# A three-stage vision tower on one core: a transposed group of values ahead of its features, and states and x on other byte offsets

## The reference

```
t = unfold3(x, stride 1)            # 27 features for each of 224*224 tokens
t = performer(t)                    # stage 1 of the kernel, out: 64 channels
t = unfold3(t, stride 2)            # 576 features, 112*112 tokens
t = performer(t)                    # stage 2, out: 64 channels
h = unfold3(t, stride 2) @ proj_w.T + proj_b          # 768 features, 56*56 tokens
                                    # stage 3: everything from here on
n = layernorm(h);  Bp, Cp = n@W_B, n@W_C;  d = softplus(n@W_D + p_Delta)
for each token t, channel c, state s (16 of them):
    a = exp(d*A);  b = (a - A)/(d*A) * d * Bp         # A is negative
    H[c,s] = a*H[c,s] + b*n[c];  y[c] = sum_s Cp[s]*H[c,s]
h = h + y
h = h + expert_mlp(layernorm(h))    # 8 experts, one per token, gelu

performer(x):  k, q, v = split(layernorm(x) @ W.T)
               kp = exp(k.w - |k|^2/2), qp likewise   # 32 features
               y = qp . (sum_t v kp) / (qp . sum kp);  y = v + proj(y);  y + mlp(layernorm(y))
```

## Time and profile before

| | us |
|---|---|
| median of three runs | 8710.51 |
| the profiled execution's own time | 8720.43 |
| its span, first to last instruction | 8718.7 |

### The profile page before, as it was taken

The page is one execution under the profiler, slowest core; times in us unless marked ns, Lnnn a source line. Parts: engine busy times, 40 slices in busy tenths (PEclk is TensorE's granted clock), DMA queues, the critical chain, the costliest instruction groups (busy, mean ns, idle before and its releaser), DMA issues.

```text
span 8718.7 us, 87074 instructions
## 1 busy us (share of the span) xinstructions
PE 7548.6 (87%) x31228; PEld 3143.8 (36%) x31228; DVE 6212.0 (71%) x6601; ACT 4308.2 (49%) x7753; POOL 5969.5 (68%) x2484
## 2 busy tenths in 40 slices
PE   8999999979999964888878888887888888888887
PEld 5444444334443321333333333333333333333333
DVE  2566666822333338888888888888888888888884
ACT  3666666833444424444544444455444445544442
POOL 0111111267666409998998999899999989999994
PEclk9999999989999976999988999988889999889988
DMA  1111111244444323323323332232333323233321
GB/s 38 38 43 45 44 44 36 51 99 100 98 101 101 66 63 106 104 95 110 114 97 121 116 105 100 100 124 95 119 107 114 104 95 124 100 107 119 114 102 52
DMA packets 356921, 786.65 MB, mean 90 GB/s; under 512 B 70437, under 2 KB 282870, under 8 KB 349000
## 3 DMA queue, kind: packets, MB, share of 16 engines
q1 hardware_dynamic: 320440, 690.78, 26.0%
q0 software_dynamic: 21712, 51.75, 2.3%
q10 hardware_dynamic: 14336, 38.54, 1.3%
HBM read 597.39 MB, written 183.35 MB: 90 GB/s over the span
## 4 chain that ended last, share of the span: by engine, by line
PE 35%; DVE 15%; ACT 6%; issue 5%; POOL 3%; DMA 0%; SPq 0%; DVEq 0%; ACTq 0%; POOLq 0%
PE ps L1644 8%; DVE v L1997 7%; PE ps L1752 6%; DVE v L1988 6%; PE ps L1651 6%; PE ps L1649 5%; PE ps L1690 3%; ACT ps L1879 3%; PE ps L1640 2%; PE ps L1755 2%; PE ps L1753 2%; POOL v L1599 1%; POOL v L1611 1%; PE ps L1694 1%; DVE dl L1978 1%
## 5 line engine op out<-in xcount | busy, mean ns | idle before, releaser
L1997 DVE TENSOR_TENSOR_SCAN v<-ps,v 128x898 f32<-128x898 f32 x1344 | 2725.3, 2028 | 92.3
L1611 POOL TENSOR_TENSOR v<-v,ct 128x1792 f32<-128x1792 f32 x672 | 2472.4, 3679 | 442.1 <-ACT st L1840 442.1
L1599 POOL TENSOR_TENSOR v<-xr,bt 128x1792 f32<-128x1792 f32 x672 | 2471.2, 3678 | 95.9 <-DMA xr<-h_by_channel 95.9
L1879 ACT ACTIVATE ps<-dr,aa 128x448 f32<-128x448 f32 x2688 | 1585.7, 627 | 1535.6 <-DVE v L1997 1518.3
L1988 DVE SCALAR_TENSOR_TENSOR v<-ps,aa,v 128x448 f32<-128x448 f32 x2688 | 1690.5, 671 | 548.1 <-ACT ps L1879 537.4
L236 POOL DMA_DIRECT2D tokens<-ob x448 | 235.3, 532 | 1534.2 <-DVE ob L563 1491.2
L1752 PE MATMUL ps<-w_or_w,gm 128*112 128x384 f32 x1792 | 716.6, 549 | 371.3 <-DVE gm L2074 278.8
L1690 PE MATMUL ps<-v,dg 128*32 128x448 f32 x5376 | 703.9, 598 | 203.6 <-POOL v L1611 109.1
L1752 PEld LDWEIGHTS ps<-w_or_w,gm 128*112 128x112 f32 x1792 | 332.8, 196 | 767.3 <-DVE gm L2074 320.5
L1644 PE MATMUL ps<-h,w_or_w 128*128 128x448 f32 x1344 | 537.2, 550 | 15.3 <-DVE gm L2041 15.3
L1805 ACT ACTIVATE h<-ps,pbias 128x448 f32<-128x448 f32 x168 | 106.2, 632 | 722.2 <-PE ps L1651 722.2
(11 more groups left out here) (322 smaller groups left out, 11960.5 us busy)
## 6 DMA issues: line engine op xcount, KB each, us to landing
xr<-h_by_channel SPq DMA_DIRECT2D x168, 896.0 KB, 7.3
dr<-delta_by_channel SPq DMA_DIRECT2D x168, 896.0 KB, 6.2
x<-tokens SPq DMA_DIRECT2D x252, 224.0 KB, 5.3
tokens<-ob POOLq DMA_DIRECT2D x448, 112.0 KB, 2.4
w_or_w<-in_w SPq DMA_DIRECT2D x29, 1536.0 KB, 6.4
w_or_w<-centred_w SPq DMA_DIRECT2D x27, 1536.0 KB, 6.5
h_by_channel<-h SPq DMA_DIRECT2D x112, 336.0 KB, 10.9
delta_by_channel<-dl SPq DMA_DIRECT2D x112, 336.0 KB, 5.1
```

What stands on the lines that cost most here:

```text
L1599: tt(v[:, n % RING, :, 1:T + 1], xr[:, dc % 2, 1:].rearrange("p (i t) -> p i t", i=4), bt[:, q:q + 1, :].to_broadcast([128, 4, T]), ALU.mu ...
L1611: tt(v[:, n % RING, :, 1:T + 1], v[:, n % RING, :, 1:T + 1], ct[:, q:q + 1, :].to_broadcast([128, 4, T]), ALU.mult).then_inc(s_cm, 1)
L1879: fn(decay(g), dr[:, dc % 2, g, :], ACT.Exp, scale=aa[:, 4 * k + g:4 * k + g + 1]).then_inc(s_a, 1)
L1997: nc.vector.tensor_tensor_scan(row, flat[:, 1024 * pair:1024 * pair + 2 * T + 2], row, 0.0, ALU.mult, ALU.add).then_inc(s_sc, 1)
```

## The change

There are two parts. In stage 2 the four matmuls that transpose the values of a pair stand first, then comes the wait for the features, and then the four that transpose the features; places in PSUM, operands and counts of instructions stay. In stage 3 the row of a group in `v` and the distance of two groups in PSUM grow from T+1 to GW = T+4 columns, the worked columns start two in instead of one, and the first state stands in column 1; `xr` becomes one tensor of 8*T+2 columns, in which x starts two columns in and the halves lie 4*T columns apart. So all four groups of v, both halves of x and all decays start 8 bytes past a multiple of 16. The scan's row starts at column 1 and has 901 columns, three unused ones between the groups. The unused columns of v are set to zero once, by two memsets more on POOL, and three engines wait for a count of 8 in place of 6 before the stage's loop. Seven one-column tensors become columns of one tensor, `small3`, which makes room.

```diff
 def transposes(n):
     own = half[1 - n % 2]
     pe.wait_ge(s_vn, n + 1)
     if n + 1 < NP:
         pe.wait_ge(s_va, n + 2)
+    for ch in range(NCH):
+        cols = slice(ch * CH, ch * CH + CH)
+        at = 256 * (ch % 2)
+        mm(ps[0:CH, 3 + ch // 2, at:at + 128], vp[:, n % RV, cols], ident[:, :], start=True, stop=True)
     pe.wait_ge(s_kp, 2 * (n + 1))
     for ch in range(NCH):
         cols = slice(ch * CH, ch * CH + CH)
-        o = ps[0:CH, 3 + ch // 2, 256 * (ch % 2):256 * (ch % 2) + 192]
-        mm(o[:, 0:128], vp[:, n % RV, cols], ident[:, :], start=True, stop=True)
-        last = mm(o[:, 128:192], kp[own, cols], ident[own, own], start=True, stop=True)
+        at = 256 * (ch % 2) + 128
+        last = mm(ps[0:CH, 3 + ch // 2, at:at + 64], kp[own, cols], ident[own, own], start=True, stop=True)
     last.then_inc(s_tr, 1)
...
+GW = T + 4
...
 def decay(g):
-    at = g // 2 * 1024 + g % 2 * (T + 1)
-    return flat[:, at + 1:at + T + 1]
+    at = g // 2 * 1024 + g % 2 * GW
+    return flat[:, at + 2:at + T + 2]
...
-xr = sb("xr", [128, 2, 4 * T + 1])
+xr = sb("xr", [128, 8 * T + 2])[:, 2:].rearrange("p (a t) -> p a t", a=2)
...
-v = sb("v3", [128, RING, 4, T + 1])
+v = sb("v3", [128, RING, 4, GW])
...
-tt(v[:, n % RING, :, 1:T + 1], xr[:, dc % 2, 1:]..., bt[...], ALU.mult)
+tt(v[:, n % RING, :, 2:T + 2], xr[:, dc % 2, :]..., bt[...], ALU.mult)
...
-row = v[:, n % RING, 2 * pair:2 * pair + 2, :].rearrange("p g t -> p (g t)")
+row = v[:, n % RING, 2 * pair:2 * pair + 2, :].rearrange("p g t -> p (g t)")[:, 1:GW + T + 2]
...
-nc.vector.tensor_tensor_scan(row, flat[:, 1024 * pair:1024 * pair + 2 * T + 2], row, 0.0, ALU.mult,
+nc.vector.tensor_tensor_scan(row, flat[:, 1024 * pair + 1:1024 * pair + GW + T + 2], row, 0.0, ALU.mult,
...
+pool.memset(v[:, :, :, T + 2:GW], 0.0).then_inc(s_set, 1)
+pool.memset(v[:, :, :, 0:1], 0.0).then_inc(s_set, 1)
...
-fn(st[:, 4 * k:4 * k + 4], v[:, n % RING, :, T], ACT.Copy).then_inc(s_st, 1)
+fn(st[:, 4 * k:4 * k + 4], v[:, n % RING, :, T + 1], ACT.Copy).then_inc(s_st, 1)
...
-fn(v[:, n % RING, :, 0], st[:, 4 * k:4 * k + 4], ACT.Copy,
+fn(v[:, n % RING, :, 1], st[:, 4 * k:4 * k + 4], ACT.Copy,
```

More of the change, by code:

```diff
@@ L1307, in decay @@
         def decay(g):
-            at = g // 2 * 1024 + g % 2 * (T + 1)
-            return flat[:, at + 1:at + T + 1]
+            at = g // 2 * 1024 + g % 2 * GW
+            return flat[:, at + 2:at + T + 2]
         def decays(pair):
-            row = flat[:, 1024 * pair:1024 * pair + 2 * T + 2]
-            return row.rearrange("p (g t) -> p g t", g=2)[:, :, 1:T + 1]
+            row = flat[:, 1024 * pair:1024 * pair + 2 * GW]
+            return row.rearrange("p (g t) -> p g t", g=2)[:, :, 2:T + 2]
         ident = sb("ident3", [128, 128])
@@ L1318, in tail @@
         desc = sb("desc", [CH, NCH, NX])
-        eps = sb("eps3", [128, 1])
-        e8 = sb("e8", [128, 1])
-        cap = sb("cap", [128, 1])
+        small = sb("small3", [128, 8])
+        eps = small[:, 0:1]
+        e8 = small[:, 1:2]
+        cap = small[:, 2:3]
         wpa = sb("wpa", [128, 3, D])
@@ L1326, in tail @@
         pbias = sb("pbias", [128, DC])
-        pm = sb("pm", [128, 1])
-        mub = sb("mub", [128, 1])
+        pm = small[:, 3:4]
+        mub = small[:, 4:5]
         wbc = sb("wbc", [128, DC, 48])
         wz = sb("wz", [128, DC, 128])
-        bbc = sb("bbc", [128, 1])
+        bbc = small[:, 5:6]
         pd = sb("pd", [128, DC])
         pc = sb("pc", [128, DC])
-        bd = sb("bd", [128, 1])
+        bd = small[:, 6:7]
         aa = sb("aa", [128, 4 * STEPS])
@@ L1511, in spread @@
                 after(sp, s_v, read)
-                sp.dma_start(xr[:, dc % 2, 1:],
+                sp.dma_start(xr[:, dc % 2, :],
                              bass.AP(xd.tensor, at, src)).then_inc(s_xr[dc % 2], 16)
@@ L1539, in _ @@
             sp.dma_start(w1, w["w1"]).then_inc(s_wv, 16)
-            sp.wait_ge(s_set, 6)
+            sp.wait_ge(s_set, 8)
             load_x(0)
@@ L1598, in weigh_in @@
                 after(pool, s_ns, n + 1 - RING)
-                tt(v[:, n % RING, :, 1:T + 1], xr[:, dc % 2, 1:].rearrange("p (i t) -> p i t", i=4), bt[:, q:q + 1, :].to_broadcast([128, 4, T]),
+                tt(v[:, n % RING, :, 2:T + 2], xr[:, dc % 2, :].rearrange("p (i t) -> p i t", i=4), bt[:, q:q + 1, :].to_broadcast([128, 4, T]),
                    ALU.mult).then_inc(s_v, 1)
@@ L1610, in weigh_out @@
                 pool.wait_ge(s_st, others(n))
-                tt(v[:, n % RING, :, 1:T + 1], v[:, n % RING, :, 1:T + 1], ct[:, q:q + 1, :].to_broadcast([128, 4, T]),
+                tt(v[:, n % RING, :, 2:T + 2], v[:, n % RING, :, 2:T + 2], ct[:, q:q + 1, :].to_broadcast([128, 4, T]),
                    ALU.mult).then_inc(s_cm, 1)
@@ L1689, in step @@
                 for g in range(4):
-                    last = mm(ps[32 * g:32 * g + 32, YB, 0:T], dg[:, 4 * k + g, :], v[:, n % RING, g, 1:T + 1],
+                    last = mm(ps[32 * g:32 * g + 32, YB, 0:T], dg[:, 4 * k + g, :], v[:, n % RING, g, 2:T + 2],
                               start=(q == 0), stop=False)
@@ L1922, in _ @@
             act.wait_ge(s_pd, 16)
-            act.wait_ge(s_set, 6)
+            act.wait_ge(s_set, 8)
             act.preload_act_table_set(BOTH)
@@ L1986, in weigh @@
                 dve.wait_ge(s_a, 4 * n + g // 2 * 2 + 2)
-                row = v[:, n % RING, g, 1:T + 1]
+                row = v[:, n % RING, g, 2:T + 2]
                 stt(row, decay(g), aa[:, 4 * k + g:4 * k + g + 1], row, ALU.subtract, ALU.mult).then_inc(s_wt, 1)
@@ L2007, in own_scan @@
                     dve.wait_ge(s_wt, 4 * n + g + 1)
-                    nc.vector.tensor_tensor_scan(decay(g), decay(g), v[:, n % RING, g, 1:T + 1],
+                    nc.vector.tensor_tensor_scan(decay(g), decay(g), v[:, n % RING, g, 2:T + 2],
                                                  0.0 if first else st[:, 4 * k + g:4 * k + g + 1], ALU.mult,
@@ L2013, in own_scan @@
                 dve.wait_ge(s_sp, 4 * owned(n) + 2 * pair - 2)
-                tt(v[:, n % RING, 2 * pair:2 * pair + 2, 1:T + 1], decays(pair),
+                tt(v[:, n % RING, 2 * pair:2 * pair + 2, 2:T + 2], decays(pair),
                    ct[:, k % Q:k % Q + 1, :].to_broadcast([128, 2, T]), ALU.mult).then_inc(s_cv, 1)
@@ L2084, in _ @@
             nc.vector.memset(ps[:, 0:AR, :], 0.0).then_inc(s_set, 1)
-            dve.wait_ge(s_set, 6)
+            dve.wait_ge(s_set, 8)
             dve.wait_ge(s_pd, 5)
```

## The result

The changed kernel takes **8673.57 us**, the median of 5 runs (8669.5 to 8674.95), beside 8710.51 for the kernel before: ratio 0.9955, interval 0.9940 to 0.9969. It is faster, by 37 us and not by 71: inside the range on record, 8608 to 8682, but outside the range of the forecast as worked out, 8622 to 8656. The profiled execution took 8669.5 us, its span is 8667.7, its mean granted clock 0.916 (before 0.918).

A forecast was written before the change was run, and what follows sets the result against it. PE was taken to bound stage 2; in stage 3 the chain, mostly PE, with POOL setting the pace for 271 us. Terms -54 - 20 + 3 = -71 us gave 8640 us for the median, range 8608 to 8682.

The forecast's parts named there:

- Transposes, -54: Stage 2's loop: grouping passes of one kind saves 0.96 us in each of 56 iterations, 54 us, all on PE's path.
- POOL, -20: Stage 3, first unit and start of the last: both multiplications at 3.38 us shorten POOL's path by 20 us.
- 271 us in which POOL sets the pace: Stage 3: 187 us in the first unit plus 84 at the last's start, where the chain runs through POOL's multiplies.
- DVE and ACT, +3: Stage 3's chain: scan +1.8 us, weighting L1988 +3.5, decays L1879 -2.3, together +3 us.
- middle units unchanged within 1 us: Sign to look for in the profile after: a unit in the middle of stage 3 keeps its length within 1 us.
- 10 us either way: Stage 3: the shifted start might move low clock stretches by 0.4 us in each of 26 units; only in the range.
- half of the transposes' gain lost: Case behind the range's upper end: stage 2 gains only half, giving 8667 us, with 10 us added for the clock.
- POOL gains nothing: Rival, stage 3: the new places undo what gave L1599 its two speeds; time 8660 us, chance 6%.
- The scan pays for its odd start: Rival, stage 3: DVE's scan from column 1 takes 0.37 us more, 100 us on the chain; 8740 us, chance 4%.
- My reading, multiples of 8: POOL's multiplications in stage 3: rows starting on a multiple of 8 bytes take 3.38 us, others 3.99.

The follow-up runs named there:

- 904 columns: The changed kernel with its scan over all 904 columns of two groups in place of 901: 8679.67 us, ratio 0.9947.
- pairs kernel: Kernel before plus regrouped transposes, x 8 bytes past 16, states in pairs of groups T+1 apart: 8668.22 us; with four extra matmuls before stage 3's projection, 8667.18.

## Why the prediction was half right

**Transposes, -54: right.** Measured -51.5 by the runs, and in the trace it takes 1118.9 us from the first pass of values to the last of features (1852.9 to 2971.8) where it took 1173.9 (1857.4 to 3031.3), 55.0 less. With the wait left where it was it takes 1119.8, so about 1 us at most is the order's, and the rest comes from passes of one kind standing together. The two kinds differ in the rows of their weights (128 and 64) and in their moving operand (128 and 64 columns); which of these counts no run separates. By the rule in the Trainium skill that the prediction weighed ("TensorE: Matmul & The Clock Gate", "Step-by-step: what each phase is for"; loads pulled ahead, so no gain) this part would have brought nothing. The trace does not agree for these passes. The features' run, estimated from a line with only 8 moving columns, was met too (0.93 us). One slip without effect: with 0.10 between the ends the term's best case is 57 us, not 58.

**POOL, -20: a term of the sum that was mis-sized.** The speeds were right (3.36 us, forecast 3.38, though from a wrong reading, below), the gain on the path was not. It gave 8.3 us in the first two units and nothing in the last. "271 us in which POOL sets the pace" took a share of the chain for a gain. The chain names what came last; how far behind it the next one was, the chain doesn't say. In the last unit that was next to nothing: in both kernels its first six steps already run at DVE's pace of 6.53 or 6.54 us. The chain before, near the end of the earlier trace rows's stretch, and the chain after at the same place:

```profile
8493.53 3.94 POOL v L1599
8497.49 1.29 DVE v L1988 x2
8498.82 0.04 issue
8498.87 2.03 DVE v L1997
```
```profile
8439.04 2.03 DVE v L2004
8441.08 1.18 DVE v L1995 x2
8442.45 1.90 issue
8445.00 1.29 DVE v L1995 x2
```

From the unit's first scan the weighting starts at 8497.49 - 8438.48 = 59.01 us before and at 8445.00 - 8386.19 = 58.81 after, both behind the eighteenth scan of the unit. A whole stretch of POOL on the chain hid 0.2 us. In the first unit the table gives the whole curve. A step of POOL is 7.69, 7.36, 7.04 or 6.72 us (the sum of its two multiplications); over 24 steps each stage of that is some 7.8 us, and unit 0 answers with 7.0, then 3.9, then nothing. After that the chain is DVE's (the kernel after, 3239 to 3427 us, unit 0 and the start of unit 1):

```profile
by line: DVE v L2004 28.9%; DVE v L1995 26.2%; issue 18.2%; ACT ps L1886 4.9%; PE ps L1656 3.9%; PE ps L1658 3.0%; PE ps L1651 2.5%; DVE dl L1985 2.0%; PE ps L1697 1.9%; PE ps L1647 1.7%; ACT dl L1839 1.4%; ACT dl L1837 1.4%; ACT dl L1832 0
```

The prediction set the floor at DVE's step of 6.53 and allowed 2 us for DVE's other work; unit 0 is 164.1 us, 7.4 over 24 steps of 6.53. What the last unit's end costs (280.2 to 281.8 in all kernels) follows no layout.

**DVE and ACT, +3, and "middle units unchanged within 1 us": the unit is right by that bound, but 0.53 us times 25 is 13.** The scan was priced by its share of the chain, +1.8 us. If all 48 of a unit count, that is 0.25 us a unit, 6 us in 25; L1879 did not get faster, and L1988 is within 1 ns of before. The other 7 us or more are on PE, as follows. Three stretches of one unit each before, and three after; the clock is the first figure behind the engines:

```profile
3841.36:4031.84 190.48, 160.19 (x571) 64.02 (x564) 167.62 (x174) 93.45 (x200) 174.73 (x49) 0.91 0.32 109
4031.84:4223.70 191.86, 161.11 (x554) 64.26 (x556) 167.66 (x174) 93.53 (x200) 174.72 (x49) 0.89 0.32 109
4223.70:4414.17 190.47, 160.14 (x571) 64.00 (x564) 167.63 (x174) 93.47 (x201) 174.72 (x49) 0.91 0.32 109
```
```profile
3775.77:3968.72 192.95, 162.41 (x554) 64.40 (x546) 167.92 (x174) 93.49 (x200) 160.04 (x48) 0.89 0.32 108
3968.72:4160.50 191.78, 161.48 (x578) 64.73 (x578) 167.84 (x175) 93.63 (x201) 159.98 (x48) 0.91 0.32 108
4160.50:4352.54 192.04, 161.19 (x554) 64.23 (x556) 167.92 (x174) 93.58 (x200) 159.96 (x48) 0.89 0.32 108
```

A unit takes about 190.5, 191.9 or 193 us. Before, 8 of 25 are of the short kind and 3 of the long; after, 2 and 7. The mean clock of a whole unit does not sort them: 191.78 us has 0.91 like 190.48, and 192.95 has 0.89 like 191.86. What sorts out the long ones is the MLP's line. Its eight passes have two prices, 4.53 and 2.77 us; the granted clock in these two stretches is 0.62 and 1.00 (the figure behind PE and weight loads), so the dear one lies in part at the lower of the clock's two levels (1.2 and 2.4 GHz), and 4.53 x 0.62 = 2.81 leaves next to nothing for another cause:

```profile
5941.11:5945.64 4.53, 4.53 (x8) 1.96 (x8) 0.62 0.81 239
5948.19:5950.96 2.77, 2.76 (x8) 1.26 (x8) 1.00 0.00 0
```

The line alone in three units running of the kernel before, the middle one long, and then over the middle units, L1752 before and L1759 after:

```profile
4414.17:4606.02 191.85, 24.92 (x62) 11.38 (x60) 0.89 0.32 108
4606.02:4798.97 192.95, 27.84 (x64) 12.59 (x64) 0.89 0.31 108
4798.97:4990.78 191.81, 25.98 (x67) 12.29 (x68) 0.91 0.32 108
```
```profile
3649.46:8438.48 4789.02, 642.00 (x1601) 297.76 (x1600) 0.90 0.32 108
```
```profile
3583.83:8386.19 4802.36, 652.19 (x1601) 301.37 (x1600) 0.90 0.32 108
```

The same passes take 10.2 us more in all. Through the 14 kernels of the table the line's time and the number of long units rise together, and the middle unit with them, from 638.8 us with 2 long units to 655.4 with 8. So the greater part of the lengthening, 10.2 of 13.3 us, is this line's passes at their dear price. It is not the amount of time at the lower level: with 904 columns the trace's clock records have 38.6 us a unit there, before 38.9 and after 40.1, and PE is busy for 4033 us, 3 more than before, yet the line has 654.1 and the unit is the longest. What counts is which work falls on the low stretches.

What makes it so is shown only in part. Every kernel with 898 or 899 columns has 191.44 to 191.81 a unit and 2 to 5 long ones, every one with 901 or more 191.98 to 192.25 and 6 to 8, with POOL slow or fast and the stage shifted or not. So it goes with the longer scan, or with the T+4 distance that always comes with it. But kernels of the same scan length differ by up to 0.37 us a unit too, more than the 0.28 that the scans' own time leaves of the 0.53, and each has one trace. Why 5 ns a scan should make long units is argued only: a unit that is 0.25 us longer can put its passes elsewhere against the low stretches. The 904 columns, 0.16 us more where the scans alone would be 0.38, show no fixed price for a column. The prediction had this effect as "10 us either way" and left it out of the sum.

In the traces POOL's 12 us too few and the middle's 10 too many make most of the 20 us between -71 and -51; the other 14 of the missing 34 are the distance of the two profiled executions from their medians (9.9 and 4.1). That the time still fell into the range is in part luck: its upper end was made from half of the transposes' gain lost and 10 us for the clock, and the first of these did not happen.

**Open.** The pairs kernel has 191.81 and 191.72 with 898 columns, the six other kernels with that length 191.44 to 191.71. In the trace this is the MLP's line again (647.1 us for before's 642.0), and before's own layout reaches 191.71 with the transposes regrouped. Whether the states' place or the faster second multiplication brings it was not separated from chance.

**Rivals.** "POOL gains nothing" was refuted as a mechanism (3.36 us), yet in the time it is the nearest: it had 8660, and the whole of stage 3's part is +8. The Trainium skill's 16-byte lines ("SBUF — State Buffer", "Specifications (TRN2)"), counted over a row, would have made both starts equal; the runs have 4.01 and 3.36. "The scan pays for its odd start" is refuted: from 901 columns on column 1, 2.033 us, from 901 on column 0, 2.035.

## What to carry to other kernels

Where PE is the bound, try matmuls of one kind in one run instead of two kinds by turns: here it was worth 0.96 us for every sixteen passes. A share of the chain is a bound, not a price: before an engine's gain is counted there, look at how late the second releaser is, and in a loop of 25 equal units price even 5 ns for each instruction of the engine that paces it. Where an edit has a part that pays and a part that costs, take the first alone: x with its one half moved by 4 bytes has most of what stage 3's part gained in the first two units and none of the longer middle, and with the transposes it made the kernel with the lowest ratio, 8655 us, 0.9928.

## What the runs showed of the hardware

- GpSimd's multiplication of 1792 columns with rows of 448 depends on where the *read* rows start against 16 bytes: all at 4 past 4.01 us, all at 8 past 3.36, by turns 8 and 12 past 3.36, by turns 8 and 0 past 3.68. So 0 and 4 past are slow (2 x 3.68 - 3.36 = 4.00 for 0), 8 and 12 fast; the mean of the four is before's 3.68. My reading, multiples of 8, was wrong for 0 and 12. The other factor was never moved.
- DVE's scan and weighting and ACT's exponentials take the same at all these starts: scans 2.26 ns a column, L1988 670 to 672 ns, L1879 627.
- On TensorE, sixteen fp32 passes with weights of 128 and 64 rows by turns cost 2.95 us, the same passes in two runs 1.99.
- Eight passes of L1752 take 4.53 us at a mean granted clock of 0.62 and 2.77 at 1.00. The mean clock alone does not tell how long a unit is: with 904 columns it has 38.6 us at the lower level and is the longest, before it has 38.9 and is 0.7 us shorter.
